# Second layer's experts on sorted, gathered blocks of 128 tokens, in place of all eight experts for every token

## The chip, the cores and the metric

One core of a Trainium2 chip runs the whole program in one launch. The metric is the device time in microseconds (us), median of several runs.

## What is computed

Four stages on x of 2048 tokens by 512: cross attention, a feed-forward layer, a second cross attention, and a mixture of experts with top 2 of 8. The change concerns the last stage, which follows a layer norm of x:

```python
logits = x @ W_gate + b_gate
_, top_idx = jax.lax.top_k(logits, TOP_K)
y_all = jax.nn.relu(jnp.einsum('bsd,edh->bseh', x, W_e) + b_e)
y = jnp.take_along_axis(y_all, top_idx[..., None], axis=2)
return y.mean(axis=2)
```

and the result is added to x. Each expert is 512x512, with a bias. The attention ahead of it has 32 heads of 16 and 8 heads of keys and values.

## The kernel before

Numbers are split in two float16 halves (high and low), and a product is three passes: high by high, high by low, low by high (`PASSES`, run by `group3`, L567). A 128x512 result over 512 inputs is so 12 matmuls. The first two stages are not touched; they end at about 1367 us.

The second layer goes tile by tile (128 tokens, two sequences of 64), 16 tiles. The order is written out by hand in a function `attn_step(n)` on each of TensorE, ScalarE (ACT) and VectorE (DVE), and semaphores tie them. For tile n: `scores` of half 0 and half 1 (16 matmuls each, L809), DVE's `less_max` (maxima L1660 and subtraction L1664), ACT's exponential and copy (L1190, L1192), DVE's `row_sums` (L1670), `reciprocals` (L1674) and `probs_lo` (L1678), `turn_p` (16 transposes, L819), ACT's `turned_p` (L1199), `weigh_v` (L830), DVE's `out_scale` (L1685), ACT's `out_hi` (L1204) and DVE's `out_lo` (L1690). The two halves share one buffer E1 and one PP1. `project(n + 1)` makes the next tile's Q and K, V; ACT's `project_hi` (L1164 to L1172) and DVE's `q_lo` (L1637), `kv_lo` (L1642 to L1651) split them; `turn_q` (L786) and `turn_k` (L793) transpose them. `turn_o` (L840) and `output(n)` end the attention of tile n, and DVE adds it to x (L1744).

Then the tile is normed: statistics (L512 to L516), root on ACT (L446, L448), four Newton operations on DVE (L434 to L440), normalisation (L525), high half on ACT (L490, `tile_hi`), low half on DVE (L485, `tile_lo`), 8 transposes (L497, `tile_turn`), store by ACT (L504, `tile_store`). `gate` gives the logits, `mask_of` (from L1607) the top two as a mask of halves. All eight experts are then run for the tile. `expert(n, e)` on TensorE is one product, 12 matmuls of 128x512:

```python
group3(banks[2 + e % 2], [(lambda p, k=k: tt[:, p, k, :], lambda p, k=k: We[e][:, p, k, :])
                          for k in range(KC)], e_mm)
```

DVE scales it and adds the bias (L1632), ACT does ReLU times the mask (L1158), and GpSimd (POOL) sums the experts (L418) and adds them to x (L421), whereupon the sync engine (SP) stores the tile (L268). Products of tile n - 2 and n - 1 stand at fixed places between the attention's pieces of tile n. POOL splits the weights of the experts (L285, L292, L294) before and during the first tile.

## Time and profile before

| what | value |
|---|---|
| median of 3 runs | 2015.8 us (2015.7 to 2016.35) |
| the profiled execution | 2015.54 us, span 2013.8 us |
| TensorE (PE) busy | 1812.5 us, 90% of the span |
| DVE busy | 1336.5 us, 66% |
| ACT busy | 892.7 us, 44% |
| POOL busy | 520.1 us, 26% |

The span goes from the first to the last instruction of the profiled execution. Busy time is the time with an instruction in the engine; PE is a matmul, PEld a load of weights. The granted clock is the share of TensorE's 2.4 GHz that it was given.

### The profile page before, as it was taken

Reading aid. Unit: us, or ns where it says so; the run is one execution under the profiler, and the core shown is the slowest. Engines: PE = TensorE matmul, PEld = TensorE weight load, DVE = VectorE, ACT = ScalarE, POOL = GpSimd, SP = SyncE. Lnnn points to the kernel's source line nnn. Section 1 sums busy time; section 2 is a strip of 40 time slices with the busy share of each in tenths; the row PEclk is TensorE's granted clock in tenths of the full one; section 3 lists DMA queues with packets and bytes.
Section 4 is the critical chain, followed back from the end, with each engine's and each line's share of the span. In section 5 each row is a group of like instructions: output and inputs, shape, how many; then the busy total and the mean of one; then the engine's idle time right before and its main releaser. Section 6 shows DMA issues by size and latency. Waiting matters only on the chain. (4 is left out here: it accounts for less than half of the span.)

```text
span 2013.8 us, 35976 instructions
## 1 busy us (share of the span) xinstructions
PE 1812.5 (90%) x14128; PEld 993.3 (49%) x14128; DVE 1336.5 (66%) x2284; ACT 892.7 (44%) x1429; POOL 520.1 (26%) x318
## 2 busy tenths in 40 slices
PE   5899998999989989999898599974799999999997
PEld 3455554554545545455454244432455555455553
DVE  5775656556565565655666877778677777787773
ACT  4353434334333433334243133323566666666662
POOL 2930304003040040300404800036032332332233
PEclk8899999999999999999999899986899999999999
DMA  5200101001010010100101300012000000000000
GB/s 205 94 12 1 53 1 53 1 2 53 1 53 1 1 54 1 53 22 1 38 1 34 132 3 1 0 42 84 1 7 12 7 7 12 7 12 7 6 12 11
DMA packets 12057, 55.26 MB, mean 27 GB/s; under 512 B 1536, under 2 KB 1536, under 8 KB 7424
## 3 DMA queue, kind: packets, MB, share of 16 engines
q1 hardware_dynamic: 11904, 53.02, 7.5%
q8 instruction: 120, 1.97, 0.4%
q14 instruction: 33, 0.27, 0.0%
HBM read 48.82 MB, written 4.19 MB: 26 GB/s over the span
## 5 line engine op out<-in xcount | busy, mean ns | idle before, releaser
L567 PE MATMUL bank<-R 128*128 128x512 f16 (+1 forms) x7152 | 1323.1, 344 | 49.2 <-DVE R L1318 18.1
L567 PEld LDWEIGHTS bank<-R 128*128 128x128 f16 x7152 | 590.5, 99 | 702.9 <-issue 54.0
L285 POOL TENSOR_SCALAR R<-R 128x2048 f32<-128x2048 f32 (+3 forms) x40 | 71.8, 1796 | 970.2 <-PE bank L567 969.2
L1318 DVE SCALAR_TENSOR_TENSOR R<-bank,biases,R 128x512 f16<-128x512 f32 x288 | 203.8, 745 | 151.2 <-ACT R L964 110.0
L418 POOL TENSOR_TENSOR R<-R 128x512 f32<-128x512 f32 x112 | 157.0, 1402 | 428.6 <-ACT R L1158 427.3
L999 ACT ACTIVATE AW<-AW 128x512 f32<-128x512 f32 x64 | 40.3, 630 | 323.3 <-DVE AW L1373 323.3
L1403 DVE SCALAR_TENSOR_TENSOR X<-bank,X 128x512 f32<-128x512 f32 x128 | 88.4, 691 | 136.2 <-PE bank L567 135.3
L294 POOL TENSOR_TENSOR R<-R 128x2048 f16<-128x2048 f32 (+2 forms) x36 | 129.6, 3601 | 3.0
L1158 ACT ACTIVATE R<-R,msk 128x512 f32<-128x512 f32 x128 | 90.3, 716 | 58.4 <-DVE R L1632 58.4
L964 ACT ACTIVATE R<-bank,biases 128x512 f16<-128x512 f32 x128 | 86.8, 682 | 66.2 <-PE bank L567 64.7
L1330 DVE SCALAR_TENSOR_TENSOR R<-bank,R 64x512 f16<-64x512 f32 x64 | 44.0, 688 | 99.7 <-ACT R L972 99.2
L1632 DVE SCALAR_TENSOR_TENSOR R<-bank,R 128x512 f32<-128x512 f32 x128 | 86.9, 680 | 28.4 <-PE bank L567 27.5
L567 PE MATMUL bank<-CT,R 128*128 128x512 f16 x384 | 89.9, 385 | 11.8 <-DVE CT L1292 11.8
L972 ACT ACTIVATE R<-bank 64x512 f16<-64x512 f32 x128 | 75.6, 591 | 55.8 <-PE bank L567 54.6
L567 PE MATMUL bank<-R,CT 128*128 128x128 f16 x1536 | 92.4, 221 | 0.0
L567 PE MATMUL bank<-AW,R 128*128 128x512 f16 x384 | 89.5, 383 | 1.1 <-ACT R L504 1.1
L567 PEld LDWEIGHTS bank<-R,CT 128*128 128x128 f16 x1536 | 89.9, 99 | 1.0
L978 ACT ACTIVATE R<-bank,biases 128x512 f16<-128x512 f32 x128 | 80.7, 684 | 0.8 <-PE bank L618 0.8
L504 ACT ACTIVATE R<-bank 128x1024 f16<-128x1024 f16 x64 | 64.4, 1016 | 34.3 <-PE bank L497 34.3
L1003 ACT ACTIVATE AW<-AW 128x512 f16<-128x512 f32 x64 | 40.3, 630 | 85.3 <-DVE AW L1384 85.0
L1389 DVE TENSOR_TENSOR AW<-AW 128x512 f16<-128x512 f32 x64 | 72.8, 1149 | 2.2
L1384 DVE SCALAR_TENSOR_TENSOR AW<-AW,smx 128x512 f32<-128x512 f32 x64 | 71.1, 1110 | 2.2
(148 smaller groups left out, 2057.6 us busy)
## 6 DMA issues: line engine op xcount, KB each, us to landing
R<-in_wB SPq DMA_DIRECT2D x16, 1024.0 KB, 5.0
R<-in_we SPq DMA_DIRECT2D x8, 1024.0 KB, 4.8
R<-in_wB SPq DMA_DIRECT2D x8, 512.0 KB, 3.7
R<-in_ctxT SPq DMA_DIRECT2D x4, 1024.0 KB, 10.0
X<-in_x SPq DMA_DIRECT2D x4, 1024.0 KB, 13.8
out<-X SPq DMA_DIRECT2D x16, 256.0 KB, 2.0
R<-in_up SPq DMA_DIRECT2D x2, 1024.0 KB, 5.5
R<-in_down SPq DMA_DIRECT2D x2, 1024.0 KB, 5.2
```

The lines of the kernel that those rows point to most:

```text
L285: g.tensor_scalar(src, src, scale, 1.0, ALU.mult, ALU.mult).then_inc(w_scaled, 1)
L294: g.tensor_tensor(lo, src, hi, ALU.subtract).then_inc(w_lo, 1)
L418: g.tensor_tensor(acc, acc, tmp[:, e % 2, :], ALU.add).then_inc(e_acc, 1)
L567: last = pe.matmul(dst, a(sa), b(sb_), start=(k == 0), stop=(k == m - 1))
L964: sc.activation(qT[:, 0, :, j, :], banks[j % 2].rearrange("p (b l) -> p b l", l=64), ACT.Identity, bias=bias_col(g * HG, j)).then_inc(p_hi, 1)
L972: last = sc.activation(V[64 * half:64 * half + 64, odd:BC:2, 0, :], v[64 * odd:64 * odd + 64], ACT.Copy, scale=UN)
L978: sc.activation(oT[:, 0, :, jb * P:(jb + 1) * P], banks[6 + jb % 2].rearrange("p (h n) -> p h n", h=HG), ACT.Identity, bias=bias_col(g, 40 ...
L1158: sc.activation(dst, tmp[:, e % 2, :], ACT.Relu, scale=msk[:, 16 + e:17 + e]).then_inc(e_rel, 1)
L1318: v.scalar_tensor_tensor(out=dst, in0=src, scalar=bias, in1=hi, op0=ALU.add, op1=ALU.subtract).then_inc(done, 1)
L1389: v.tensor_tensor(PPb[:, blocks(hf), 1, :], Eb[:, blocks(hf), :], PPb[:, blocks(hf), 0, :], ALU.subtract).then_inc(s_plo, 1)
L1403: v.scalar_tensor_tensor(out=xt, in0=banks[4 + t % 2], scalar=UN2, in1=xt, op0=ALU.mult, op1=ALU.add).then_inc(y_add, 1)
L1632: v.scalar_tensor_tensor(out=tmp[:, e % 2, :], in0=banks[2 + e % 2], scalar=UN, in1=beb[:, e, :], op0=ALU.mult, op1=ALU.add).then_inc(e_bi ...
```

## The change

The experts leave the tiles. Each token gets two lists: its lower and its higher chosen expert. In each list the tokens are sorted by expert, each expert's part is filled up to whole blocks of 128, and 22 blocks are reserved per list, 44 in all, a fixed number.

- Per tile, POOL's `route` builds one-hot rows of the two experts (M16), TensorE's `rank` multiplies them by a triangle and by ones, which counts in bank 2 how many tokens of that expert came before; DVE's `rank_of` picks the rank, and POOL turns it into block and row, as two one-hot tiles of 128x128 per list. TensorE's `table` adds their product to a table of tokens by position.
- SP stores per tile x with the attention added, in the output, and the two halves of the normed tile, in a DRAM scratch `xn_rows` (`rows_out`). ACT waits for the latter store of the tile before it writes the next high half (`ffn_hi`). 512 rows of padding ahead of both are written with zeros first.
- After the last tile DVE works out which expert each block has and TensorE, ACT and DVE the 128 token numbers of each block (16 steps of `c_step`).
- Then 44 blocks: POOL gathers 128 rows of 2 KB by indirect DMA (four buffers), TensorE transposes them (`block_turn`), ACT stores them, TensorE loads the block's expert and bias place into registers and multiplies (`block_product`: one matmul for the bias, 12 of 128x512), ACT does ReLU times a half, and POOL adds the rows to the output in DRAM by an indirect DMA with addition. Before the second list's first addition, POOL waits for all of the first's.
- In `attn_step` the order changes on all three engines: `output(n - 1)` now opens tile n; DVE adds it and norms it between the two halves; `project_hi`, `q_lo` and `kv_lo` of the next tile come before `out_hi` and `out_scale` of half 1.
- POOL splits the last four experts' weights one by one ahead of the routing of tiles 0 to 3, in pieces of 512 columns.

```diff
+NB = 22
+ROUND = 12582912.0
+BLOCKS = LISTS * NB
...
+            def rows_out(n):
+                sp.wait_ge(a_add, n + 1)
+                xt = X[:, n, :] if isinstance(n, int) else X[:, ds(n, 1), :].rearrange("p a d -> p (a d)")
+                sp.dma_start(out[ds(n * P + PAD, P), :], xt).then_inc(out_done, 16)
+                sp.wait_ge(n_lo, n * 2 + 36 if not isinstance(n, int) or n < NT - 2 else 49 + n)
+                sp.dma_start(xnr[ds(n * P + PAD, P), :], R4[:, 0:1024]).then_inc(xn_out, 16)
...
+                g.tensor_copy(idxf, idx8[:, 0:2]).then_inc(rt_f, 1)
+                pool.wait_ge(rt_f, n + 1)
+                g.tensor_scalar(eAB[:, 0:1], idxf[:, 0:1], idxf[:, 1:2], 1.0, ALU.min, ALU.mult).then_inc(rt_step, 1)
+                g.tensor_scalar(eAB[:, 1:2], idxf[:, 0:1], idxf[:, 1:2], 1.0, ALU.max, ALU.mult).then_inc(rt_step, 1)
+                step(2)
+                for l in range(LISTS):
+                    g.tensor_scalar(M16[:, par, l * NE:(l + 1) * NE], iota8, eAB[:, l:l + 1], 1.0,
+                                    ALU.is_equal, ALU.mult).then_inc(rt_m, 1)
...
+                g.tensor_tensor(row2, rank2, lbm, ALU.add).then_inc(rt_step, 1)
+                step(9)
+                w(pool, tt_mm, n)
+                for l in range(LISTS):
+                    g.tensor_scalar(hot_key[:, l, :], iota128, key[:, l:l + 1], tok1, ALU.is_equal, ALU.mult).then_inc(rt_hot, 1)
+                    g.tensor_scalar(hot_row[:, l, :], iota128, row2[:, l:l + 1], 1.0, ALU.is_equal, ALU.mult).then_inc(rt_hot, 1)
+                g.tensor_scalar(tok1, tok1, float(P), 1.0, ALU.add, ALU.mult).then_inc(rt_step, 1)
...
+            def gather(b):
+                g.indirect_dma_start(GX[b % 4], None, xnr, bass.IndirectOffsetOnAxis(bidx[:, b:b + 1], 0)).then_inc(g_in[b % 4], 16)
+            def scatter(b):
+                g.indirect_dma_start(out, bass.IndirectOffsetOnAxis(bidx[:, b:b + 1], 0), OB[b % 4], None,
+                                     compute_op=ALU.add).then_inc(o_out[b % 4], 16)
...
+            for b in range(BLOCKS):
+                if b == NB:
+                    for i in range(4):
+                        pool.wait_ge(o_out[i], 16 * len(range(i, NB, 4)))
+                pool.wait_ge(blk_rel, b + 1)
+                scatter(b)
+                if b + 4 < BLOCKS:
+                    pool.wait_ge(blk_turned, b + 1)
+                    gather(b + 4)
...
             def output(n):
                 pe.wait_ge(a_toev, n + 1)
-                group3(banks[0], [(lambda p, qu=qu: oT1[:, 2 * p + qu // 2, qu % 2, :], lambda p, qu=qu: Wo1[:, p, qu, :])
...
                 one, two, more = has(n, 1), has(n, 2), has(n, -1)
+                if one:
+                    output(n - 1)
                 scores(n, 0)
-                if two:
-                    expert(n - 2, 6, T2[buf])
                 scores(n, 1)
-                if two:
-                    expert(n - 2, 7, T2[buf])
                 if one:
                     tile_turn(pe, ffn_stat(n - 1), 0, 7, ffn_turn(n - 1))
                 turn_p(n, 0)
                 if one:
-                    gate(n - 1, T2[1 - buf])
-                    expert(n - 1, 0, T2[1 - buf])
+                    gate(n - 1, T2[0])
+                weigh_v(n, 0)
                 if more and not n_is_first(n):
                     pe.wait_ge(r_lg, n)
                     tile_turn(pe, attn_stat(n + 1), 1, 7, attn_turn(n + 1))
-                weigh_v(n, 0)
-                if one:
-                    expert(n - 1, 1, T2[1 - buf])
                 turn_p(n, 1)
+                if two:
+                    table(n - 2)
                 if n_is_first(n):
                     weigh_v(n, 1)
                     tile_turn(pe, attn_stat(1), 1, 7, attn_turn(1))
                 if more:
-                    project(n + 1, ctx_t, T2[buf])
-                else:
-                    expert(n - 1, 2, T2[1 - buf])
+                    project(n + 1, ctx_t, T2[1])
                 if not n_is_first(n):
                     weigh_v(n, 1)
-                if one:
-                    expert(n - 1, 2 if more else 3, T2[1 - buf])
                 if not more:
                     pe.wait_ge(r_lg, n)
                 turn_o(n)
+                if one:
+                    rank(n - 1, 1 - par)
                 if more:
                     turn_q(n + 1)
-                if one:
-                    expert(n - 1, 3 if more else 4, T2[1 - buf])
-                if more:
                     pe.wait_ge(b_on, n * 2 + 2)
                     turn_k(n + 1)
-                output(n)
-                if one and more:
-                    expert(n - 1, 4, T2[1 - buf])
-                if one:
-                    expert(n - 1, 5, T2[1 - buf])
...
+            def block_product(b, i):
+                col = pe.value_load(boff[0:1, ds(b, 1)] if not isinstance(b, int) else boff[0:1, b:b + 1],
+                                    min_val=0, max_val=(NE - 1) * 4096)
+                row = pe.value_load(boff[0:1, ds(b + BLOCKS, 1)] if not isinstance(b, int)
+                                    else boff[0:1, BLOCKS + b:BLOCKS + b + 1], min_val=0, max_val=(NE - 1) * P)
+                w(pe, blk_rel, b - 1)
+                pe.wait_ge(blk_store, b + 1)
+                dst = banks[i % 2]
+                pe.matmul(dst, pick[:, ds(row, P)], beHL, start=True, stop=False)
+                for k in range(KC):
+                    for sa, sb_ in PASSES:
+                        last = pe.matmul(dst, TB[i % 2][:, sa, k, :], WeAll[:, ds(col + (sb_ * 2048 + k * D), D)],
+                                         start=False, stop=(k == KC - 1 and (sa, sb_) == PASSES[-1]))
+                last.then_inc(blk_mm, 1)
...
-                    norm_store(ffn_turn(n - 1), 1 - buf)
-                if two:
-                    expert(n - 2, 7)
+                    norm_root(act, ffn_stat(n - 1), 0)
+                    ffn_hi(n - 1)
                 turned_p(n, 0)
                 exponentials(n, 1)
+                if one:
+                    norm_store(ffn_turn(n - 1), 0)
+                out_hi(n, 0)
                 if more and not n_is_first(n):
-                    norm_store(attn_turn(n + 1), buf)
-                out_hi(n, 0)
-                if one:
-                    expert(n - 1, 0)
-                    expert(n - 1, 1)
+                    norm_store(attn_turn(n + 1), 1)
                 turned_p(n, 1)
                 if n_is_first(n):
                     norm_root(act, attn_stat(1), 1)
                     tile_hi(act, attn_stat(1), 1, yn)
-                    norm_store(attn_turn(1), buf)
...
+            def block_store(b):
+                act.wait_ge(blk_turned, b + 1)
+                w(act, blk_mm, b - 1)
+                sc.activation(TB[b % 2], banks16[4 + b % 2].rearrange("p (s k n) -> p s k n", s=2, k=KC), ACT.Copy).then_inc(blk_store, 1)
+            def block_relu(b):
+                act.wait_ge(blk_mm, b + 1)
+                w(act, o_out[b % 4], 16 * (b // 4))
+                sc.activation(OB[b % 4], banks[b % 2], ACT.Relu, scale=UN * 0.5).then_inc(blk_rel, 1)
+            block_store(0)
+            for b in range(BLOCKS):
+                if b + 1 < BLOCKS:
+                    block_store(b + 1)
...
+            def attn_step(n, par):
                 one, two, more = has(n, 1), has(n, 2), has(n, -1)
                 less_max(n, 0)
                 if n_is_first(n):
                     y_stats(NT - 1)
-                if two:
-                    expert(n - 2, 5)
+                if one:
+                    x_add(n - 1)
+                row_sums(n, 0)
+                reciprocals(n, 0)
+                if one:
+                    norm_apply(dve, ffn_stat(n - 1), 0, x_tile(n - 1), yn)
+                probs_lo(n, 0)
+                less_max(n, 1)
                 if one:
                     ffn_lo(n - 1)
-                if two:
-                    expert(n - 2, 6)
-                row_sums(n, 0)
-                reciprocals(n, 0)
-                probs_lo(n, 0)
-                if two:
-                    expert(n - 2, 7)
-                less_max(n, 1)
                 if n_is_first(n):
                     y_norm(NT - 1)
-                if one:
-                    mask_of(n - 1)
                 row_sums(n, 1)
...
                 out_lo(n, 0)
                 reciprocals(n, 1)
+                if one:
+                    mask_of(n - 1)
                 if n_is_first(n):
                     y_add_to_x(NT - 1)
                     norm_stats(dve, attn_stat(1), 1, x_tile(1), True)
                     norm_apply(dve, attn_stat(1), 1, x_tile(1), yn)
                     tile_lo(dve, attn_stat(1), 1, yn)
-                if one:
-                    expert(n - 1, 1)
                 if has(n, -2):
                     norm_stats(dve, attn_stat(n + 2), 1, x_tile(n + 2), True)
+                if more:
+                    q_lo(n + 1)
+                    kv_lo(n + 1)
                 out_scale(n, 1)
                 out_lo(n, 1)
-                if more:
-                    q_lo(n + 1)
-                if one:
-                    expert(n - 1, 2)
-                if more:
-                    kv_lo(n + 1)
                 if has(n, -2):
                     norm_apply(dve, attn_stat(n + 2), 1, x_tile(n + 2), yn)
                     tile_lo(dve, attn_stat(n + 2), 1, yn, attn_turn(n + 1) + 1)
                 if one:
-                    expert(n - 1, 3)
-                dve.wait_ge(a_y, n + 1)
...
```

How the instructions stand. **DVE, inside a tile, from half 0's subtraction to the low half of the normed tile.** Before:

```order
L1664 TENSOR_TENSOR R<-bank,smx 128x512 [waits b_max]
...
L1632 SCALAR_TENSOR_TENSOR R<-bank,R 128x512 [waits e_acc]
...
L485 TENSOR_TENSOR R<-yn,R 128x512 [waits n_turned]
...
L1670 TENSOR_REDUCE smx<-R 128x16 [waits b_exp]
L1674 RECIPROCAL smx<-smx 128x16 [waits b_sum]
L1678 SCALAR_TENSOR_TENSOR R<-R 128x16x64 [waits b_phi]
...
L1660 TENSOR_REDUCE smx<-bank 128x8 [waits b_s]
```

Now:

```order
L1859 TENSOR_TENSOR R<-bank,smx 128x512 [waits b_max]
...
L1890 SCALAR_TENSOR_TENSOR X<-bank,X 128x512
L669 BN_STATS stat<-X 128x6 [waits a_add]
...
L1865 TENSOR_REDUCE smx<-R 128x16 [waits b_exp]
L1869 RECIPROCAL smx<-smx 128x16 [waits b_sum]
...
L591 TENSOR_TENSOR stat<-stat 128x1 [waits n_r0]
...
L682 TENSOR_SCALAR yn<-X,stat 128x512 [waits n_r]
L1873 SCALAR_TENSOR_TENSOR R<-R 128x16x64 [waits b_phi]
...
L1855 TENSOR_REDUCE smx<-bank 128x8 [waits b_s]
...
L642 TENSOR_TENSOR R<-yn,R 128x512 [waits n_turned]
```

The addition (L1890), the statistics and the normalisation (L682) of tile n - 1 came in, and its low half (L485, now L642) moved behind the second half's maxima.

**TensorE, from the tile's first transposes to Q's projection.** Bank 7's transposes are those of a normed tile, g1w is the gate. Before:

```order
L497 MATMUL bank<-ident,R 128x128 [waits n_stored]
...
L819 MATMUL bank<-ident,R 128x128 [waits b_plo]
...
L567 MATMUL bank<-g1w,R 128x8 [waits n_stored]
...
L567 MATMUL bank<-R 128x512 [waits e_bias]
...
L497 MATMUL bank<-ident,R 128x128 [waits n_stored,n_lo]
...
L830 MATMUL bank<-R 128x16 [waits b_tev]
```

Now:

```order
L654 MATMUL bank<-ident,R 128x128 [waits n_stored]
...
L975 MATMUL bank<-ident,R 128x128 [waits b_plo]
...
L724 MATMUL bank<-g1w,R 128x8 [waits n_stored]
...
L986 MATMUL bank<-R 128x16 [waits b_tev]
...
L654 MATMUL bank<-ident,R 128x128 [waits n_stored,n_lo]
...
L975 MATMUL bank<-ident,R 128x128 [waits b_tev,b_plo]
...
L1027 MATMUL bank<-R 128x128 [waits rt_hot]
```

The expert's product is gone, and weighing V (now L986) stands ahead of the second normed tile's transposes.

## Rows read from the trace of the kernel before

**Rows 1.** The page, part 2: granted clock in 40 slices, in tenths.
```profile
PEclk8899999999999999999999899986899999999999
```
**Rows 2.** Timeline of tile 3, TensorE: start us, us, engine, line, operation, count [idle before].
```profile
1500.58 0.41 PE L809 MATMUL bank<-R 48*128 48x64 f16 x16
1500.91 2.76 PE L567 MATMUL bank<-R 128*128 128x512 f16 x12
...
1508.99 1.07 PE L819 MATMUL bank<-ident,R 128*128 128x128 f16 x16 [1.49 <-DVE R L1678]
1509.90 0.45 PE L567 MATMUL bank<-g1w,R 128*128 128x8 f16 x12
...
1513.23 0.95 PE L830 MATMUL bank<-R 128*128 128x16 f16 x32
...
1520.11 1.47 PE L567 MATMUL bank<-AW,CT 128*128 128x256 f16 x12
...
1537.07 0.41 PE L809 MATMUL bank<-R 48*128 48x64 f16 x16
```
**Rows 3.** Stretches: window, length, busy PE, PEld, DVE, ACT, POOL, clock, DMA.
```profile
1360.00:1380.00 20.00, 13.87 (x100) 7.46 (x98) 13.32 (x25) 5.86 (x13) 11.70 (x6) 0.93 0.14 46
1380.00:1400.00 20.00, 3.52 (x64) 3.00 (x64) 19.53 (x21) 6.35 (x8) 19.37 (x8) 0.50 0.17 59
...
1420.00:1440.00 20.00, 11.42 (x102) 6.76 (x103) 15.58 (x38) 11.54 (x15) 0.00 (x0) 0.74 0.00 1
...
1500.00:1537.00 37.00, 35.30 (x323) 19.70 (x321) 27.85 (x59) 24.36 (x40) 11.70 (x9) 1.00 0.03 9
```
**Rows 4.** Timeline of tile 3, ACT and DVE.
```profile
1503.67 1.06 ACT L1190 ACTIVATE R<-R 128x1024 f32<-128x1024 f32 x1 [2.91 <-DVE R L1664]
...
1510.20 1.92 ACT L1199 ACTIVATE R<-bank 128x1024 f16<-128x1024 f16 x2
...
1516.76 0.41 DVE L1685 TENSOR_TENSOR R<-bank,smx 128x256 f32<-128x256 f32 x1
...
1523.20 0.58 ACT L1164 ACTIVATE R<-bank 128x512 f16<-128x512 f32 x1
...
1526.55 0.26 DVE L1651 COPY R<-R 128x384 f16<-128x384 f16 x1
```
**Rows 5.** Timeline of tiles 0 and 1, where no experts stand between.
```profile
1378.27 0.61 PE L809 MATMUL bank<-R 48*128 48x64 f16 x16 [1.21 <-ACT R L1185]
...
1402.98 1.89 PE L819 MATMUL bank<-ident,R 128*128 128x128 f16 x16 [12.53 <-DVE R L1678]
...
1409.99 1.03 PE L497 MATMUL bank<-ident,R 128*128 128x128 f16 x8 [2.06 <-DVE R L485]
...
1412.13 4.13 PE L567 MATMUL bank<-AW,R 128*128 128x512 f16 x12 [1.12 <-ACT R L504]
...
1423.66 0.69 DVE L1744 SCALAR_TENSOR_TENSOR X<-bank,X 128x512 f32<-128x512 f32 x1 [0.77 <-PE bank L567]
...
1425.06 0.41 PE L809 MATMUL bank<-R 48*128 48x64 f16 x16 [1.43 <-ACT R L1185]
...
1425.75 0.20 ACT L446 ACTIVATE stat<-stat 128x1 f32<-128x1 f32 x1 [0.84 <-DVE stat L516]
...
1427.45 1.28 DVE L1660 TENSOR_REDUCE smx<-bank 128x8 f32<-128x512 f32 x2
...
1431.18 1.22 DVE L1670 TENSOR_REDUCE smx<-R 128x16 f32<-128x1024 f32 x1 [0.53 <-ACT R L1190]
...
1433.68 1.27 DVE L1660 TENSOR_REDUCE smx<-bank 128x8 f32<-128x512 f32 x2
```
**Rows 6.** POOL's groups by form: x count, busy, mean ns, idle before.
```profile
L294 POOL TENSOR_TENSOR R<-R 128x2048 f16<-128x2048 f32 x26 | 107.5, 4135 | 2.2
...
L292 POOL TENSOR_SCALAR g1w<-R 128x32 f16<-128x32 f32 x1 | 0.2, 217 | 0.2 <-POOL R L285 0.2
```
**Rows 7.** DMA issues: operation, count, KB each, median us to landing.
```profile
out<-X SPq DMA_DIRECT2D x16, 256.0 KB, 2.0
```

## What was predicted, blind

> **What bounds the kernel now.** I read the page, then the stretches, then the timeline of one tile. TensorE is busy for 90% of the span, and its granted clock is at 0.9 or more of its full speed in nearly every slice [rows 1]. The change touches the last part alone: sixteen tiles of attention with the experts woven in, from tile 0's scores at 1378.3 to the end at 2013.8. There a tile takes 36.5 us (scores at 1500.6 and 1537.1), and a product with one expert is 12 matmuls in 2.76, or 2.6 from start to start [rows 2]. Eight are 20.7 of the 36.5; what is left for TensorE is some 15. From 1500 to 1537 it is busy 35.3 us of 37, DVE 27.9, ACT 24.4 [rows 3]. So TensorE bounds the stage, because experts fill every gap that the attention chain leaves. Where none do (tile 0, 1380 to 1400) it is busy 3.5 of 20 and the granted clock is 0.50: its lower level, 1.2 GHz [rows 3]. That is what a tile looks like with its filling taken out, and it is the question of this change.
>
> **What goes.** 16 x 8 products, 16 x 20.7 = 331 us of TensorE; eight additions with bias on DVE and eight ReLUs on ACT per tile; POOL's sums. Had TensorE stayed full, the 44 new blocks (8 transposes, 13 matmuls: 0.5 + 2.8 = 3.3 each, 145 in all) would give back 186 less some 60 of new tail. The order of the tile decides otherwise.
>
> **The tile after, as one chain.** I put every instruction of the new step on its engine in order, with durations of this trace. The same done for the old step closes at 36.7 against 36.5, so the method holds. From the start of tile n's scores, in us:
> - scores, row maxima, subtraction: 3.1 (1500.58 to ACT's 1503.67) [rows 2, 4]. Then DVE alone, in a row: adding the previous tile's output and its statistics 2.1; row sums, reciprocal and low half of the probabilities 2.5; Newton's steps and the normalisation 1.2 (1425.75 to 1427.45, less 0.5 of ACT's root) [rows 5]; the second half's maxima and subtraction 2.5; low half of the normalised tile 0.7 (as one 128x512 DVE row). Now 12.2, since transposes of P stand on TensorE behind those of that tile.
> - 8 and 16 transposes, 1.03 and 1.89 at the lower clock [rows 5]: 15.2. Before, ffn_lo stood ahead of the second half's maxima, and P's transposes began 8.4 after the scores, not 13 [rows 2].
> - ACT copies them (1.92), and only behind that does the second half's exponential and copy (two of 1.06) [rows 4]; the norm's store, half of such a pair, 1.0: 20.2. gate and weighing V, 0.45 and 0.95 [rows 2]: 21.6.
> - DVE scales, ACT rounds, DVE takes the rest (0.42 each), logits: 23.5, because the next transposes wait for the logits. 8 + 16 transposes and the table's two matmuls: 26.4.
> - Q's 12 matmuls cost 4.13 in tile 0, after a gap, where 2.75 is the row at the full clock [rows 5]; K and V 1.47, weighing 0.95: 32.7, overlaps counted. ACT's copies of Q, K, V and, behind the last, DVE's low half and copy of K take 3.6 (1523.20 to 1526.8), and 0.4 to start: 36.7 [rows 4]. Only then the second half is scaled, rounded, split: 38.1. Before, that stood ahead of Q's low half.
> - transposes of O, Q, K at the lower clock 3.6; output's 12 matmuls 4.0: 45.7, and the next scores stand behind them.
>
> So **45.7 us a tile, 9 more than now**, with TensorE waiting for more than half. Its gaps there are 8 us (scores to the first transposes), 5, 2 and 5. The rows on which I take the lower clock: transposes after gaps of 12.5 and 2.1 us took 1.89 and 1.03 [rows 5]. All at the full clock (8 transposes 0.45, 16 in 0.9, 12 wide matmuls 2.6) the chain is 39.8, all at half of it 49.3; I take the mixed sum, as tile 0 shows just that mix. The granted share agrees: 0.74 from 1420 to 1440, where TensorE was busy 11.4 us of 20 [rows 3], and here it is 22 of 45.7. No engine is near its limit (DVE 21.4, ACT 18.7, TensorE 22). POOL's routing per tile is some 18 small operations, 0.22 each and about 0.2 between dependent ones [rows 6]: 6.5, hidden, as its result is wanted a step later. SP's two stores per tile (256 KB, 2.0 us to landing [rows 7]) hide too; ACT waits for one of them a step later. If that cover were gone, each would add its 2.
>
> **Tile 0 and the start.** Stages before don't change. Expert splits 2 and 3 in finer pieces cost POOL perhaps 4 us more, hidden in its wait for the previous stage. Tile 0 took 46.8 (1378.27 to 1425.06 [rows 5]) with POOL's splits slowing DVE; fewer fall there now: I take 40 (bounds 36 and 47). The later splits, three, fall in tiles 1 to 3: 0 to 10 us in all, counted in the range.
>
> **The tail.** After tile 15's scores: 26.4 without Q's projection, but with weighing; its O path and output to 34.5; addition, statistics, root, Newton, norm 3.9; halves, transposes, store, gate, top two 4.9: 43.3. POOL's first part 2.0, rank and DVE 1.0, POOL's second part 4.3 (seven dependent steps, four one-hot tiles), table, copy, value matmul, two DVE steps 2.0: 53. First gather issued and landed 4 (guess from [rows 7], twice), its transposes and store 2: **59**. Now nothing of this is hidden: the products with eight experts stood here, 20.7 and their last sums.
>
> **The blocks.** Per block two indirect DMAs are issued by POOL, of 128 rows of 2 KB, one of them adding in DRAM. This trace has no such instruction. Below: they hide, and TensorE's 3.3 rules. Above: POOL needs for each what its longest row takes, about 4.1 (the split of 128x2048 [rows 6]), so 8.4 a block with waits. I take what is nearest, the same 256 KB on SP, 2.0 from issue to landing [rows 7], for each of the two in series: 4.0, with waits 4.2. 44 x 4.2 = 185. Halfway POOL waits until all of the first list's adds have landed: 5. Last ReLU, add and landing: 4.
>
> The Trainium skill, DMA: Bandwidth & Descriptors, section Latency and other measured facts, gives a register load from memory a floor of about 0.6 us. TensorE does two per block between its transposes and its product; exposed, they would make the block 3.3 + 1.2 = 4.5 and the sum 13 us more. No row here shows one. The same page, section Anatomy of one DMA, gives a POOL-issued DMA a fixed 2.0 us, mostly completion; by that the block would be TensorE's 3.3, since four buffers cover the latency, and the sum 40 less.
>
> **Sum**: 1378 + 40 + 14 x 45.7 (640) + 59 + 185 + 9 = 2311. The profiled execution took 2015.54 at a span of 2013.8, and the median of the runs is 2015.8, so 2 are added: **2313**.
>
> **Rivals.**
> - *The clock holds.* As the dense runs (transposes, projection) lie close enough, TensorE stays at 2.4 GHz: 39.8 a tile. 2313 less 15 x 5.9 = 2225 (fourteen tiles, and the tail as one). For: 0.93 granted from 1360 to 1380, where the engine was busy 13.9 us of 20 [rows 3]. Against: the slow transposes after gaps of 2 us [rows 5]. Chance 0.15.
> - *POOL bounds the blocks.* 7 to 8.4 a block: 2436 to 2498. For: everything in the block loop's order goes through POOL's queue, scatter of b ahead of gather of b + 4. Against: nothing here. Chance 0.15.
> - *The tiles fall to the busiest engine.* If the new order lets tile n + 1's start overlap tile n's end, the step goes to DVE's sum, 21.4, plus some waits. With the blocks at 3.3 (145), faster than now needs a tile below (2013.8 - 1378 - 40 - 59 - 145 - 9) / 14 = 27.3; it decides from there. For: the sums. Against: scores of n + 1 need K and Q transposed, and these the low halves, all late in the chain. At 25 it is 1981 + 2 = 1983. Chance 0.04.
> - *It doesn't do what it says*, for instance runs fewer blocks. 44 are fixed in number, whatever the data; so only a change that leaves the time within 4 us for another reason is left, 2014 to 2018, chance 0.01.
> - The forecast: 0.65.
>
> **How the numbers follow.** A difference under 0.2% (4 us) is about what a measurement of this kernel can't tell from none. The likeliest case gives 2313. The range takes in the clock that holds (2225), and on the other side 7 us a block (2436), with 10 for the splits: 2220 to 2440. Outside are most of 8.4 a block, and the faster case. Faster 0.04, same 0.01, slower 0.95.
>
> **What would show it.** In the changed profile: scores 45 us apart from tile 2 on; TensorE busy about half of a tile with a granted clock between 0.5 and 0.8; P's transposes 15 us after the scores, waiting for DVE's low half of the normed tile; 59 us between the last scores and the first block's transposes; then blocks 4.2 apart, TensorE or POOL without gaps. The prediction is wrong if tiles are under 37 apart, if a block takes over 8, or if the wait at P's transposes is not there.

## The result, and the profile after

The changed kernel takes **2270.0 us** (three executions, 2268.7 to 2270.4; a fourth took 6533 us, no trace shows why, and it is left out) against 2016.1 for the kernel before: a ratio of 1.126, 95% interval 1.1235 to 1.1279. The forecast was 2313, range 2220 to 2440, slower with a chance of 0.95.

The profiled execution has a span of 2268.3 us. Its page, parts 1 and 2 (engine, busy us and share, instructions; then tenths of 40 equal slices):

```profile
PE 1727.1 (76%) x13582; PEld 995.7 (44%) x13583; DVE 1205.8 (53%) x2143; ACT 877.2 (39%) x1390; POOL 577.2 (25%) x647
...
PE   5799989999999999989789984543454344535887
...
PEclk8899999999999999999899996666566666766999
```

In thirteen slices, the second attention stage, TensorE reads 3 to 5, and the granted clock is 0.5 to 0.7, where it was 0.9 or more from the second tile on [rows 1]. That is the picture of tile 0 [rows 3] spread over sixteen tiles. One tile of the changed kernel, TensorE's timeline:

```profile
1625.24 0.61 PE L965 MATMUL bank<-R 48*128 48x64 f16 x16
1628.57 0.41 PE L965 MATMUL bank<-R 48*128 48x64 f16 x16 [2.71 <-DVE R L1859]
1637.44 1.03 PE L654 MATMUL bank<-ident,R 128*128 128x128 f16 x8 [8.47 <-DVE R L642]
1638.27 1.91 PE L975 MATMUL bank<-ident,R 128*128 128x128 f16 x16
1645.15 0.48 PE L724 MATMUL bank<-g1w,R 128*128 128x8 f16 x12 [4.97 <-ACT R L661]
1645.49 1.00 PE L986 MATMUL bank<-R 128*128 128x16 f16 x32
1648.29 1.01 PE L654 MATMUL bank<-ident,R 128*128 128x128 f16 x8 [1.80 <-DVE lgt L1811]
...
1651.02 3.76 PE L724 MATMUL bank<-AW,R 128*128 128x512 f16 x12
...
1662.05 1.03 PE L996 MATMUL bank<-ident,R 128*128 128x128 f16 x8 [5.17 <-DVE R L1885]
...
1668.79 0.41 PE L965 MATMUL bank<-R 48*128 48x64 f16 x16
```

What to see are the four waits of 8.47, 4.97, 1.80 and 5.17 us, three on DVE and one on ACT; the forecast's were 8, 5, 2 and 5. The stretch of this tile (columns as in [rows 3]): TensorE is busy for 20.9 of 44 us at a clock of 0.64, where it was busy 35.3 of 37 [rows 3]:

```profile
1625.00:1669.00 44.00, 20.88 (x243) 15.57 (x244) 19.85 (x46) 18.80 (x31) 3.23 (x9) 0.64 0.03 13
```

The sum of the forecast against the trace (the scores' start times cut the stage):

| term | forecast | measured | from |
|---|---|---|---|
| start of the stage | 1378 | 1356.0 | first scores |
| tile 0 | 40 | 39.9 | to 1395.82 |
| fourteen tiles | 14 x 45.7 = 640 | 14 x 44.64 = 625.0 | 1395.82 to 2020.81 |
| last scores to the first block | 59 | 56.7 | to 2077.50 |
| 44 blocks and their end | 185 + 9 | 190.8 | to 2268.3 |
| span | 2311 | 2268.3 | |

Half of the 43 us between the sums is in the first line, in a part of the program that the forecast took as unchanged.

Set against the kernel before, the 254 us lie in two places: the fourteen tiles take 106 us more (625.0 against 518.7), and what stands behind the last scores 178 more (247.5 against 70.0, from 1943.79 to the end at 2013.8). The start and tile 0 give 29 back.

### The profile page after: what moved, and what is told of

It reads as the page before. It is cut to its first block, busy times and chain, and to the rows that moved or that the text cites. A ratio compares the mean times of both kernels' runs of the same rounds, so it can differ in the third digit from the quotient of the medians.

```text
span 2268.3 us, 35407 instructions
## 1 busy us (share of the span) xinstructions
PE 1727.1 (76%) x13582; PEld 995.7 (44%) x13583; DVE 1205.8 (53%) x2143; ACT 877.2 (39%) x1390; POOL 577.2 (25%) x647
## 4 chain that ended last, share of the span: by engine, by line
PE 63%; DVE 18%; ACT 9%; issue 7%; DMA 2%; POOL 1%; DVEq 0%; ACTq 0%; POOLq 0%; SPq 0%
PE bank L724 47%; PE bank L1123 4%; PE bank L975 2%; PE bank L775 2%; PE bank L654 2%; DVE smx L1855 2%; DVE AW L1593 1%; PE bank L761 1%; PE bank L943 1%; DVE R L642 1%; DVE R L1859 1%; PE bank L986 1%; DMA R<-xn_rows,R 1%; ACT R L1396 1%; DVE R L1873 1%
## 5 line engine op out<-in xcount | busy, mean ns | idle before, releaser
L724 PE MATMUL bank<-R 128*128 128x512 f16 (+1 forms) x5616 | 969.3, 334 | 42.3 <-DVE R L1522 14.7
L724 PEld LDWEIGHTS bank<-R 128*128 128x128 f16 x5616 | 445.3, 99 | 530.3 <-issue 51.6
L654 PE MATMUL bank<-ident,R 128*128 128x128 f16 x512 | 52.6, 269 | 184.0 <-DVE R L642 159.1
L654 PEld LDWEIGHTS bank<-ident,R 128*128 128x128 f16 x512 | 40.6, 121 | 194.0 <-issue 134.1
L1123 PE MATMUL bank<-R 128*128 x528 | 123.9, 386 | 0.0
L1169 ACT ACTIVATE R<-bank,biases 128x512 f16<-128x512 f32 x128 | 86.9, 682 | 68.9 <-PE bank L724 67.5
L1396 ACT ACTIVATE R<-bank 128x1024 f16<-128x1024 f16 x64 | 62.0, 1020 | 113.7 <-PE bank L975 113.7
L349 POOL TENSOR_TENSOR R<-R 128x2048 f16<-128x2048 f32 (+2 forms) x28 | 96.8, 3458 | 2.3
L1865 DVE TENSOR_REDUCE smx<-R 128x16 f32<-128x1024 f32 x32 | 38.9, 1215 | 87.5 <-ACT R L1387 87.5
L565 POOL DMA_INDIRECT out<-R x44 | 69.8, 1586 | 60.8 <-ACT R L1471 57.8
L661 ACT ACTIVATE R<-bank 128x1024 f16<-128x1024 f16 x64 | 64.4, 1016 | 46.7 <-PE bank L654 46.6
```

The source lines that it names most:

```text
L349: g.tensor_tensor(lo, src, hi, ALU.subtract).then_inc(w_lo, 1)
L565: g.indirect_dma_start(out, bass.IndirectOffsetOnAxis(bidx[:, b:b + 1], 0), OB[b % 4], None, compute_op=ALU.add).then_inc(o_out[b % 4], 16)
L654: last = pe.transpose(banks16[bank][:, sk * P:(sk + 1) * P], xs[:, par, sk // KC, (sk % KC) * P:(sk % KC + 1) * P], ident)
L661: nc.scalar.activation(dst, banks16[bank][:, 0:2 * KC * P].rearrange("p (a n) -> p a n", a=2 * KC), ACT.Copy).then_inc(n_stored, 1)
L724: last = pe.matmul(dst, a(sa), b(sb_), start=(k == 0), stop=(k == m - 1))
L1123: last = pe.matmul(dst, TB[i % 2][:, sa, k, :], WeAll[:, ds(col + (sb_ * 2048 + k * D), D)], start=False, stop=(k == KC - 1 and (sa, sb_) ...
```

## Experiments

Tile periods below are the distance from tile 1's to tile 15's scores, divided by 14: 37.05 in the kernel before (1425.06 to 1943.79), 44.64 in the changed one. A whole time without an interval (e2, e3, e4, e6 to e9) is that of one execution; the kernels that were repeated here stayed within 0.5%, and the smallest difference that is read from a single one is 1%.

**e1: where the 22 us at the start come from.** The kernel before, with the changed kernel's short pieces for the expert weights. (The change splits all eight experts in pieces of 512, not the last four alone.)

```diff
-                split(40 + m, raw[:, (37 + m) % 2, :], *halves(...))
+                split_fine(40 + m, raw[:, (37 + m) % 2, :], *halves(...), WS)
```

> The kernel before, with one edit: GpSimd splits the eight experts' weights of the second layer in pieces of 512 columns, as the changed kernel does, instead of 2048. Theory A (the changed kernel's 22 us earlier start of the stage, 1355.96 against 1378.27, comes from the short pieces alone, which hold VectorE up less): the stage's first scores at 1356 to 1358, and the whole at 1990 to 1996, since later splits beside tile 0 get cheaper too. Rival B (the earlier start comes from something else that the change moved, such as the memory layout or the freed additions): 2015 to 2017, the first scores at 1378.

Measured: 1989.5 us, ratio 0.987 (0.985 to 0.990), first scores at 1356.43. Theory A holds (the whole half a us under its range): the pieces alone bring the start to within 0.5 us of the changed kernel's. The mechanism stands in the timeline of the kernel before, in a stretch that the forecast had not read, POOL, DVE and TensorE at 1117 and from 1141:

```profile
1117.06 4.38 POOL L294 TENSOR_TENSOR AW<-R,AW 128x2048 f16<-128x2048 f32 x1
1118.21 3.78 DVE L1555 TENSOR_TENSOR R<-R 128x512 f16<-128x512 f32 x1 [0.69 <-ACT R L1107]
...
1141.48 4.05 POOL L294 TENSOR_TENSOR R<-R 128x2048 f16<-128x2048 f32 x1
1141.63 3.92 DVE L438 TENSOR_SCALAR cstat<-cstat 128x4 f32<-128x4 f32 x1
...
1149.88 4.10 POOL L294 TENSOR_TENSOR R<-R 128x2048 f16<-128x2048 f32 x1
1150.00 5.13 DVE L485 TENSOR_TENSOR R<-R 128x512 f16<-128x512 f32 x2
...
1154.59 1.89 PE L497 MATMUL bank<-ident,R 128*128 128x128 f16 x16 [12.78 <-DVE R L485]
```

DVE's subtraction of 128x512 takes 0.69 us when undisturbed. Here it takes 3.78 and ends half a us after POOL's subtraction of 2048 columns. At 1141.63 even an operation on 128x4 numbers takes 3.92, where e1 has 0.17 for it, and TensorE stands idle for 12.78 us behind a chain of such operations. In the changed kernel's timeline the same chain runs beside pieces of 512:

```profile
1141.42 2.62 DVE L642 TENSOR_TENSOR R<-R 128x512 f16<-128x512 f32 x2
1142.54 0.62 PE L654 MATMUL bank<-ident,R 128*128 128x128 f16 x8 [2.26 <-DVE R L642]
```

The Trainium skill has this as a rule (SBUF — State Buffer, section Who interferes with whom): VectorE and GpSimd share one pair of ports, and whichever issues first gets it for its whole instruction while the other is fully blocked; on VectorE's side this goes for its two-port modes, and for an instruction with two inputs in the SBUF against a GpSimd instruction that reads it. The trace agrees for the subtraction, whose inputs both lie there: it ends at 1121.99, POOL's at 1121.44.

**e5, e12, e11: how long a piece may be.** If a hold-up lasts as long as the piece, the length is the dose. The kernel before with all its splits cut, not the experts' alone, into 512, 1024 and 256 columns. (The earliest splits were in pieces of 512 already: e12 leaves them so, e11 cuts them to 256 too.)

```diff
+                cuts = [slice(a, min(a + 512, src.shape[1])) for a in range(0, src.shape[1], 512)]
...
-                g.tensor_tensor(lo, src, hi, ALU.subtract).then_inc(w_lo, 1)
+                for q in cuts:
+                    last = g.tensor_tensor(lo[:, q], src[:, q], hi[:, q], ALU.subtract)
+                last.then_inc(w_lo, 1)
```

> The kernel before with every split of weights on GpSimd in pieces of 512 columns (experiment e1 did that for the second layer's eight experts alone and took 1989.5). Theory A (a GpSimd operation of 2048 columns holds up whatever VectorE operation meets it, so it costs wherever VectorE is on the path): the splits between 1088 and 1135 meet VectorE too (three subtractions of 3.8 us there instead of 0.7 in e1's trace), with TensorE waiting 8 us behind one of them; 6 to 12 us less than e1, 1977 to 1984. The splits of the first layer's groups lie in a stage where TensorE is busy 93 to 97% and give 0 to 5 more. Rival B (more and shorter instructions make GpSimd late, and the weights arrive later than TensorE wants them): 1989 to 2000.

> The kernel before with every split outside those that were already fine in pieces of 1024 columns (2048: 2015.8, 512: 1940.2). Theory A (the hold-up is as long as a piece): about a third to a half of the 75 us is gained, 1975 to 1992, and the longest VectorE 128x512 subtraction in the stage at 1090 to 1150 is about 2 us where it is 3.8 with pieces of 2048. Rival B (any cut at all frees VectorE, as the gain came from the shorter queue): 1940 to 1950.

> The kernel before with every split on GpSimd in pieces of 256 columns (512: 1940.2). Theory A (a VectorE operation can be held up for as long as one GpSimd piece lasts, and from 512 on that is no longer than what the chain has in hand): 1932 to 1942. Rival B (twice as many instructions, each with its own start, make GpSimd late, since a piece of 512 takes 0.69 us where a quarter of a 2048 takes 0.5): over 1945, with TensorE waiting for weights.

One DVE line, its 32 subtractions of 128x512, each with its durations in ns (min/median/max) and first and last start. In the kernel before:

```profile
L1555 DVE TENSOR_TENSOR R<-R x32: 691/692/3783, 1089.7 to 1331.1; 128x512 f16<-128x512 f32 x32
```

In e12, pieces of 1024:

```profile
L1562 DVE TENSOR_TENSOR R<-R x32: 691/692/1839, 1051.9 to 1283.5; 128x512 f16<-128x512 f32 x32
```

In e5, pieces of 512:

```profile
L1562 DVE TENSOR_TENSOR R<-R x32: 691/693/1127, 1043.1 to 1269.2; 128x512 f16<-128x512 f32 x32
```

In e11, pieces of 256:

```profile
L1562 DVE TENSOR_TENSOR R<-R x32: 691/693/1010, 1029.4 to 1253.3; 128x512 f16<-128x512 f32 x32
```

| piece | POOL's subtraction, mean | DVE's longest | first scores | whole, ratio to before |
|---|---|---|---|---|
| 2048 | 4.14 | 3.78 | 1378.3 | 2015 |
| 1024 | 2.26 | 1.84 | 1323.1 | 1958.3, 0.972 (0.970 to 0.973) |
| 512 | 1.27 | 1.13 | 1305.6 | 1940.2, 0.962 (0.961 to 0.964) |
| 256 | 0.75 | 1.01 | 1286.2 | **1926.9**, 0.956 (0.955 to 0.958) |

The longest subtraction falls with the piece, as theory A has it. The sizes were missed, all on one side: 1977, 1975 and 1932 were the lowest expected. I had priced the stage at 1100 and forgotten the first layer, where TensorE "is busy 93 to 97%". From 0 to 1000 us it is busy 956 us in e5 and 925 in e1; the waits sat in the 3 to 7% that I had passed over. The 256 case beats both kernels by 4.4% and 15%, with the same arithmetic as before.

In the 256 case POOL's own time begins to count. Its first scores come 19.5 us earlier than with 512, but the whole is only 13.3 faster, as its tile 1 takes 48.2 us (38.1 with 512). POOL, DVE, SP's queue and TensorE there:

```profile
1323.86 5.23 POOL L300 TENSOR_TENSOR R<-R 128x256 f16<-128x256 f32 x8
1329.11 0.33 SPq L264 DMA_DIRECT2D R<-in_be  x1
1336.08 1.29 DVE L1667 TENSOR_REDUCE smx<-bank 128x8 f32<-128x512 f32 x2 [8.14 <-DMA R<-in_be]
1338.75 0.61 PE L816 MATMUL bank<-R 48*128 48x64 f16 x16 [13.54 <-DVE R L1671]
```

SP loads the experts' biases (6.9 us to landing) only when POOL's last split has ended, and DVE waits 8.14 us for them. With 512 that load went out at 1339.2, 9.5 us ahead of tile 1's scores, and nothing waited for it.

**e2: the order in the tile.** The changed kernel with the transposes of P ahead of those of the normed tile.

```diff
+                turn_p(n, 0)
                 if one:
                     tile_turn(pe, ffn_stat(n - 1), 0, 7, ffn_turn(n - 1))
-                turn_p(n, 0)
-                if one:
                     gate(n - 1, T2[0])
```

> The changed kernel with TensorE's transposes of the first half's probabilities ahead of the previous tile's transposes, not behind. Theory A (the tile is one chain, and the 12.2 us from scores to the first transposes are on it): probabilities are ready 3.2 us earlier, ScalarE's copies and exponentials move with them, tile 41.2 instead of 44.6, the whole at 2215 to 2230. Rival B (the 8.5 us gap is only where TensorE happens to wait, and the chain runs elsewhere): 2265 to 2272, the time reappearing as a longer wait before the gate or before the transposes of O.

Measured: 2201.9 us, 40.25 a tile: theory A, and at 4.4 us more than the 3.4 it had. TensorE's timeline of a tile whose scores begin at 1603.03:

```profile
1606.35 0.41 PE L965 MATMUL bank<-R 48*128 48x64 f16 x16 [2.71 <-DVE R L1858]
1612.04 1.89 PE L975 MATMUL bank<-ident,R 128*128 128x128 f16 x16 [5.27 <-DVE R L1872]
1615.23 1.03 PE L654 MATMUL bank<-ident,R 128*128 128x128 f16 x8 [1.31 <-DVE R L642]
1618.90 0.48 PE L724 MATMUL bank<-g1w,R 128*128 128x8 f16 x12 [2.63 <-ACT R L661]
```

P's transposes begin 9.0 us after the first scores instead of 13.0, and the gate 15.9 instead of 19.9, because ACT copies P, does the exponentials and reaches the norm's store 4 us earlier.

**e3: the clock.** Idle matmuls in the gaps keep TensorE at work: the 30 shown, and 16, 5 and 18 in the three later gaps.

```diff
+            def fill(m):
+                for j in range(m):
+                    pe.matmul(banks[3], ident, Wq1[:, 0, j % KC, :], start=True, stop=True)
...
+                w(pe, a_add, n)
+                fill(30)
                 if one:
                     tile_turn(pe, ffn_stat(n - 1), 0, 7, ffn_turn(n - 1))
```

> The changed kernel with 69 idle matmuls of 128x512 per tile (nobody reads their result) in TensorE's four gaps: 30 ahead of the previous tile's transposes, 16 ahead of the gate, 5 and 18 further on. Theory A (the low granted clock is 5 to 6 us of the tile's 44.6): at the upper clock the 69 take 14.9 us and lie in the gaps, the granted clock goes over 0.9, transposes of 16 take 0.9 instead of 1.9, wide products of 12 take 2.6 to 2.8, and the tile falls to 39 to 40: the whole at 2195 to 2210. Rival B (the clock costs nothing on the path): the tile stays at 44 to 46, 2260 to 2290. If the clock stays low, the fillings take 29 us, overrun the gaps, and the tile is over 50: then nothing is said.

Measured: 2213.3 us, 40.37 a tile, a little above theory A's 39 to 40. The stretch of one tile (window, length, busy PE, PEld, DVE, ACT, POOL, clock, DMA share, GB/s) has a granted clock of 0.96:

```profile
1646.00:1685.00 39.00, 31.37 (x299) 17.38 (x300) 20.14 (x48) 18.57 (x32) 5.86 (x17) 0.96 0.04 15
```

TensorE's timeline of that tile:

```profile
1659.50 1.06 PE L975 MATMUL bank<-ident,R 128*128 128x128 f16 x16
...
1670.33 2.76 PE L724 MATMUL bank<-AW,R 128*128 128x512 f16 x12
...
1682.20 2.75 PE L724 MATMUL bank<-AW,R 128*128 128x512 f16 x12
```

Sixteen transposes take 1.06 us instead of 1.91, Q's projection 2.76 instead of 3.76 (2.8 to 4.4 over the tiles), and the tile falls by 4.3. Matmuls that compute nothing make the kernel 57 us faster. That the low clock cost time on the path is thereby shown; it is 4.3 of the tile, net of what the fillings themselves hold up, where the forecast had 5.9 between its mixed and its warm chain (45.7 and 39.8).

**e4: the old order with its filling taken out.** Only the first of each product's 12 matmuls is left, so this kernel leaves out eleven twelfths of the experts' products; the eight additions and ReLUs per tile stay.

```diff
-                group3(banks[2 + e % 2], [(lambda p, k=k: tt[:, p, k, :], lambda p, k=k: We[e][:, p, k, :])
-                                          for k in range(KC)], e_mm)
+                pe.matmul(banks[2 + e % 2], tt[:, 0, 0, :], We[e][:, 0, 0, :], start=True, stop=True).then_inc(e_mm, 1)
```

> The kernel before with each product with an expert cut from 12 matmuls to the first one of them (eleven twelfths of the second layer's expert products left out; the additions of bias, ReLUs and sums stay). It asks what the old order's tile is with its filling taken out. Theory A (the changed kernel's order, with the previous output and its norm ahead of the probabilities, is what costs 4 us or more of the tile): 37 to 40 a tile, so about the old 36.5 or little over, the whole at 2000 to 2060. Rival B (the filling alone held the clock and the old order is as slow without it): 43 to 46 a tile, the whole at 2110 to 2160. Rival C (the old chain was shorter than its TensorE work): under 34 a tile, 1960 or less.

Measured: 2008.4 us, 37.45 a tile. The stretch of one tile (columns as above):

```profile
1611.00:1649.00 38.00, 23.97 (x232) 15.36 (x232) 28.14 (x59) 23.91 (x39) 11.16 (x8) 0.68 0.02 8
```

The granted clock is 0.68, near the changed kernel's 0.64. Of 19 us of matmuls taken out of each tile, none came back: 37.45 against 37.05. The experts' products lay in the gaps of the old attention chain, and without them that chain, at the low clock, is as long as the full tile was. How long it is at the full clock no run shows.

Since the old step closes at 37.45 at the low clock, with the experts' additions and ReLUs that the changed kernel no longer has, the clock alone does not make 44.64. 7.2 of the 7.6 us that a tile lost come with the new step: its order, and what it adds (ranks, table, stores). e2 shows 4.4 for one place of the order; the rest is not taken apart.

**e9: order and clock together.** The edits of e2 and e3, with 53 idle matmuls.

> The changed kernel with the edits of e2 and e3 together: probabilities' transposes first, and 53 idle matmuls per tile in TensorE's gaps (18, 4, 8, 5 and 18). Tiles were 44.6 apart in the changed kernel, 40.3 with the first edit, 40.4 with the second. Theory A (order and clock are two separate costs of one chain): both are saved, 35.5 to 37 a tile, the whole at 2130 to 2160. Rival B (they save the same wait twice): 39.5 to 40.5 a tile, the whole at 2190 to 2205.

Measured: 2171.8 us, 37.63 a tile: 7.0 of the 8.7 us that the two saved apart. That is outside both ranges, and much nearer to theory A. A part of the rest is in two tiles of 44.4 and 43.9 us: there TensorE stands idle for 5.3 and 5.8 us ahead of and inside the output product, for nothing that the profile shows (1.90 and 2.03 in two tiles of the changed kernel). The twelve others average 36.6. Another part is the filling itself: in one tile P's low half is ready at 1635.89 and its transposes start at 1637.02, behind 18 idle matmuls that took 6.3.

**e6, e7, e8: what a block waits for.** The changed kernel's timeline of one block, TensorE, ACT and POOL:

```profile
2140.36 0.61 PE L1109 MATMUL bank<-ident,R 128*128 128x128 f16 x8
2140.56 0.60 ACT L1471 ACTIVATE R<-bank 128x512 f32<-128x512 f32 x1 [2.65 <-PE bank L1123]
2141.06 1.02 ACT L1466 ACTIVATE R<-bank 128x1024 f16<-128x1024 f16 x1
2141.44 1.59 POOL L565 DMA_INDIRECT out<-R  x1 [1.28 <-ACT R L1471]
2141.91 0.10 PEld L1120 LDWEIGHTS bank<-R,CT 128*128 x1 [1.11 <-issue]
2141.91 0.39 PE L1120 MATMUL bank<-R,CT 128*128 128x512 f16 x1 [0.94 <-ACT R L1471]
...
2142.14 2.75 PE L1123 MATMUL bank<-R 128*128 x12
```

Between the end of the transposes (2140.97) and the product there is 0.94 us; over the 44 blocks such gaps are 23.6 us, 0.54 each. The view names ACT's ReLU, which had ended at 2141.16, long before; the two register loads of the block stand in just that place and are not in the view. e6 fixes the two numbers when the program is built (the tokens then go through experts that they did not choose), e7 moves the loads, e8 moves ACT's copy to DVE.

```diff
-                col = pe.value_load(boff[0:1, ds(b, 1)] ...)
-                row = pe.value_load(boff[0:1, ds(b + BLOCKS, 1)] ...)
+                col, row = (i % 8) * 4096, (i % 8) * P
```
```diff
+                    at = block_loads(i * 4 + k)
                     block_turn(i * 4 + (k + 1), k + 1)
-                    block_product(i * 4 + k, k)
+                    block_product(i * 4 + k, k, at)
```
```diff
-                sc.activation(TB[b % 2], banks16[4 + b % 2]..., ACT.Copy).then_inc(blk_store, 1)
+                v.tensor_copy(TB[b % 2], banks16[4 + b % 2]...).then_inc(blk_store, 1)
```

> The changed kernel with TensorE's two register loads per block taken away: block b takes the weights and the bias of expert b mod 4 (or so), fixed when the program is built, not of the expert that the block's tokens chose. Same transfers, same matmuls. Theory A (the gap of about 0.75 us between the transposes of the next block and the product, in a block of 4.13, is the two loads): 3.4 a block, the stretch of 44 blocks 33 us shorter, the whole at 2235 to 2245. Rival B (ScalarE's copy behind its ReLU is what the product waits for, 1.1 us after the transposes end): 4.1 a block stays, 2262 to 2272. Rival C (transfers bound it, DMA engines are busy 73%): a fall to 3.8 at most.

> The changed kernel with the two register loads of a block put ahead of the next block's transposes, not between these and the product. Theory A (a load costs only where the engine's instructions ahead of it are short): the product of the block before covers them, 3.5 a block, the whole at 2240 to 2250. Rival B (a load holds the queue wherever it stands): 4.1 a block, 2265 to 2272.

> The changed kernel with the copy of a block's transposed tokens on VectorE, which is idle then, in place of ScalarE (1.02 us, behind a ReLU of 0.6). Theory A (the register loads set the block): nothing, 2262 to 2272. Rival B (ScalarE's ReLU and copy in a row set it): 0.6 less a block, 26 us, 2240 to 2246.

The 352 transposes of the blocks, with first and last start in us. In the changed kernel:

```profile
L1109 PE MATMUL bank<-ident,R x352: 218/219/312, 2077.5 to 2252.4; 128*128 128x128 f16 x176
```

In e6:

```profile
L1109 PE MATMUL bank<-ident,R x352: 219/219/314, 2078.1 to 2229.6; 128*128 128x128 f16 x176
```

In e7:

```profile
L1109 PE MATMUL bank<-ident,R x352: 216/219/315, 2075.4 to 2228.6; 128*128 128x128 f16 x176
```

In e8:

```profile
L1109 PE MATMUL bank<-ident,R x352: 218/219/315, 2077.0 to 2250.5; 128*128 128x128 f16 x176
```

Divided by 43, a block takes 4.07, 3.52, 3.56 and 4.03 us. Without the loads, and with the loads ahead of the transposes, it is the same; the copy on DVE changes nothing (2268.9 us). So the loads are 0.5 us of each block, and behind a product's matmuls they are hidden: 2245.8 us in e7 for moving two instructions up. e6 took 2246.9, 2 us above its theory A. In e7 TensorE is busy for 145.4 of the 154 us from 2075 to 2229, 3.3 a block; its matmuls wait 11.0 us in all for gathered rows, 7.7 in the changed kernel, so part of that wait lay behind the loads.

**e10: sorting, rid of all this.** All splits in pieces of 512, and the edits of e9 and e7.

> The changed kernel with all that helped so far: every split on GpSimd in pieces of 512, probabilities' transposes first, idle matmuls in the gaps, register loads ahead of the transposes. It asks whether sorting pays once it is rid of these costs; the kernel before with short pieces took 1940.2. Sum: first scores 1305.6 (as there), tile 0 42, 14 tiles of 36 (504), 56 to the first block, 44 blocks of 3.55 (156), 9: 2073, with 2 around it 2075. Theory A (the tile's chain and the tail stay, so the sorted form loses whatever is mended): 2050 to 2100. Rival B (with the clock up and the chain short, tiles fall towards VectorE's 21 us of work): under 30 a tile, 1990 or less.

Measured: 2092.1 us, ratio 1.039 (1.037 to 1.040), 37.49 a tile. Theory A. Against e5, which has the same splits and all eight experts for each token, it is 152 us slower. The tiles no longer differ (37.49 against 37.1 in e5); from the last scores to the end it is 220.4 us (1868.89 to 2089.3) against 71.6 (1868.45 to 1940.0).

## Why the prediction was right, and where it was not

- **What bounds the tile.** Right, in mechanism and size: with the filling gone the tile is one chain over three engines. Its steps, from tile 6's scores at 1625.24: first transposes at 12.2 (forecast 12.2), gate at 19.9 (20.2), transposes of the next norm at 23.1 (23.5), of O at 36.8 (38.1), next scores at 43.6 (45.7; 44.64 over fourteen tiles).
- **The two causes.** The forecast named "one chain" and the lower clock together. e2 and e3 show both, 4.4 and 4.3 us a tile, and e9 gets 7.0 from the two. e4 adds that the low clock is not enough: with it the old step needs only 37.45. The step that laid a cost on P's transposes standing behind those that wait for ffn_lo was right. ("15 us after the scores" among its signs does not fit its own chain, which has 13; 13.0 was measured.)
- **The clock's size.** "Q's 12 matmuls cost 4.13" and output's 4.0 were taken for every tile from tile 0 [rows 5]. They were 2.8 to 5.3, 3.8 and 3.4 in the tile shown: most of the 1.1 us a tile, 15 in all, that the term was too large.
- **The start of the stage.** Here a step failed: "Stages before don't change. Expert splits 2 and 3 in finer pieces cost POOL perhaps 4 us more, hidden". The pieces were priced for POOL alone; e1 shows that DVE got 22 us back. The forecast had the same fact in hand for tile 0 ("with POOL's splits slowing DVE") and did not carry it to the stage ahead.
- **The tail.** 59 against 56.7; right. The 59 holds 2 us for the first block's transposes and store, which the trace has behind that point; up to it the forecast is 57, with the first gather at 53 (53.0 measured) and its rows 3.7 us later (4).
- **The blocks.** 4.2 against 4.1 us, for the wrong reason: this agreement is luck. "2.0 from issue to landing, for each of the two in series" made 4.0. POOL in fact needs 0.99 to issue the gather and 1.59 for the scatter, waits for ACT ahead of 42 of the 44 scatters, and isn't the bound; TensorE's 3.3, the register loads (0.55 by e6) and waits for gathered rows are 4.07. So neither TensorE nor POOL is "without gaps". The Trainium skill's floor of 0.6 us for a register load (DMA: Bandwidth & Descriptors, section Latency and other measured facts) was weighed by the forecast at 1.2 a block. That the two loads cost time there is what e6 and e7 show; what they cost is 0.55 for both, and no run shows what one load takes by itself. The fixed 2.0 us of a transfer, covered by four buffers (the Trainium skill, same page, section Anatomy of one DMA), would make 3.3; without the loads the runs give 3.5.
- **The rivals.** The clock didn't hold; e3 shows about what it would have been, 40.4 a tile with the fillings in it, where the rival had 39.8. POOL did not bound. The tile did not fall to the busiest engine: even with order and clock mended (e9) it takes 37.6, far from the 27.3 that would have decided.

## What to carry to other kernels

Work that lies in the gaps of a dependent chain can be free: taking it away gave nothing back here (e4; the clock fell with it), and doing it later, alone, costs all of itself, here 191 us of blocks and 57 of tail. Before replacing dense work by less but later work, close the chain without it and compare that length with what you hope for. And long GpSimd instructions beside a VectorE chain are a cost of their own: look in the trace for VectorE operations far above their median, and cut the GpSimd ones until these are gone (2015 to 1927 us here), watching what waits for GpSimd's end, since short pieces make it slower.

## What the hardware showed that I had not expected

- GpSimd's pieces: its subtraction of 256 columns takes 0.75 us, of 2048 4.14, so eight short ones are 45% dearer than the long one, and the kernel is 4.4% faster. POOL is then busy for 655 us of the span (520 before) and late once: a load behind its last split holds DVE for 8.14 us.
- Two register loads on TensorE cost 0.5 us a block between short transposes and a product, and nothing behind twelve wide matmuls.
- An indirect DMA keeps POOL for 0.99 us (gather of 128 rows) and 1.59 us (scatter with addition); the DMA engines are busy 67% of the block stretch.
- The 69 idle matmuls a tile raise the granted clock from 0.64 to 0.96, and the tile is 4.3 us shorter.
